# Halving the experts' weights inside the experts' stage of a perceiver layer, without a copy in memory

## The reference

```
logits = router(x @ wqkv.T)                     # N x 8
top_logits, idx = top_k(logits, 2)
scores = softmax(top_logits)
for each row and each of its 2 experts e:
    a, g = split(x_row @ w1[e].T, 2)            # 704 and 704 values
    out_row += score * ((silu(a) * g) @ w2[e].T)
```

## Time and profile before

| | us |
|---|---|
| median of 3 runs | 1886.67 (1884.86 to 1888.04) |
| the profiled execution | 1884.02 |
| its span, first to last instruction | 1882.2 |
| PE busy | 1736.2 (92%) |
| DVE busy | 1387.1 (74%) |
| ACT busy | 1307.0 (69%) |
| POOL busy | 1293.4 (69%) |

### The profile page before, as it was taken

One profiled execution on the slowest core, in us unless ns is written; L12 is line 12 of the kernel. 1 busy time (PEld: TensorE's weight loads), 2 busy tenths in 40 slices (PEclk: granted clock), 3 DMA queues, 4 the chain that ended last, 5 costly groups with the idle time before them and its releaser, 6 DMA issues. The chain is left out here.

```text
span 1882.2 us, 59167 instructions
## 1 busy us (share of the span) xinstructions
PE 1736.2 (92%) x24673; PEld 1146.0 (61%) x24673; DVE 1387.1 (74%) x3579; ACT 1307.0 (69%) x1610; POOL 1293.4 (69%) x669
## 2 busy tenths in 40 slices
PE   6899999999999999999999999999778993699996
PEld 3566666666666666666666666666534672588885
DVE  7788888888888888888888888788766566544443
ACT  5588788888878888878888878888664442233332
POOL 3488888898888888898898888888652100243442
PEclk9999999999999999999999999999898785799998
DMA  8544445444445544445554545554166674688884
GB/s 274 157 119 121 128 113 156 130 127 112 131 117 151 136 129 112 131 117 146 138 132 111 132 117 142 134 138 104 51 215 203 202 236 148 241 248 254 267 245 119
DMA packets 170923, 290.83 MB, mean 155 GB/s; under 512 B 56162, under 2 KB 138466, under 8 KB 170434
## 3 DMA queue, kind: packets, MB, share of 16 engines
q1 hardware_dynamic: 163170, 276.83, 50.6%
q0 software_dynamic: 7488, 10.23, 2.7%
HBM read 169.80 MB, written 33.16 MB: 108 GB/s over the span
## 5 line engine op out<-in xcount | busy, mean ns | idle before, releaser
L420 POOL TENSOR_TENSOR pl<-pT,ph 128x1024 f16<-128x1024 f32 x416 | 881.7, 2132 | 188.4 <-ACT ph L462 188.2
L679 DVE CUSTOM_DVE_ANT_0 junk<-ring,mbias 128x804 bf16<-128x804 f32 x496 | 491.5, 991 | 155.7 <-issue 150.1
L460 ACT ACTIVATE pT<-score,small 128x1024 f32<-128x1024 f32 (+1 forms) x416 | 464.5, 1117 | 68.0 <-PE score L485 34.0
L462 ACT ACTIVATE ph<-score,small 128x1024 f16<-128x1024 f32 (+1 forms) x416 | 464.5, 1117 | 0.0
L883 PE MATMUL ring<-cp,wkp 128*128 128x402 f16 x1536 | 309.0, 338 | 10.2 <-DVE kst L758 3.3
L894 PE MATMUL ring<-wvp,cp 128*128 128x256 f16 (+1 forms) x2496 | 306.3, 274 | 2.9 <-DVE v L664 1.7
L894 PEld LDWEIGHTS ring<-wvp,cp 128*128 128x128 f16 (+1 forms) x2496 | 233.7, 99 | 78.4 <-issue 21.8
L623 POOL TENSOR_TENSOR cp<-cx,cp 128x804 f16<-128x804 f32 x128 | 252.9, 1996 | 21.5 <-ACT cp L792 21.5
L800 ACT ACTIVATE kh<-ring,small 128x402 f16<-128x402 f32 x256 | 155.2, 606 | 154.9 <-PE ring L883 154.9
L908 PE MATMUL ring<-kh,qm 32*128 32x402 f16 x992 | 253.1, 334 | 4.9 <-DVE mx L679 0.3
L507 PE MATMUL o_acc<-v,pl 128*128 128x33 f16 (+1 forms) x3328 | 240.2, 178 | 0.0
(11 more groups left out here) (243 smaller groups left out, 2098.5 us busy)
## 6 DMA issues: line engine op xcount, KB each, us to landing
cx<-in_ctxT SPq DMA_DIRECT2D x32, 1601.0 KB, 6.7
w1p<-wsp SPq DMA_DIRECT2D x24, 1408.0 KB, 8.0
kst<-kh SPq DMA_DIRECT2D x256, 100.5 KB, 2.9
msk<-in_mask SPq DMA_DIRECT2D x64, 400.2 KB, 5.5
kst<-kh SPq DMA_DIRECT2D x256, 99.6 KB, 2.5
wsp<-w_parts SPq DMA_DIRECT2D x24, 704.0 KB, 5.8
w2p<-wsp SPq DMA_DIRECT2D x24, 640.0 KB, 4.3
kst<-kl SPq DMA_DIRECT2D x128, 100.5 KB, 2.7
```

The costliest lines, as they stand in the source:

```text
L420: pool.tensor_tensor(pl[:, u].rearrange("p h q -> p (h q)"), pT[:, u], ph[:, u].rearrange("p h q -> p (h q)"), ALU.subtract).then_inc(pl_r ...
L460: act.activation(pT[0:n, u].rearrange("k (h a q) -> k a h q", a=2, q=S), scored, ACT.Exp, bias=lift[0:n, 0:1], scale=SSCALE)
L462: act.activation(ph[0:n, u].rearrange("k h (a q) -> k a h q", a=2), scored, ACT.Exp, bias=lift[0:n, 0:1], scale=SSCALE).then_inc(exp_done, 1)
L679: dve.tensor_tensor_reduce(junk[:, n % 2], made[:, :, 0:KW], mbias[:, j, 2 * KW * half:2 * KW * half + 2 * KW].rearrange("p (c k) -> p c k ...
```

## The change

The round trip through `wsp` goes. The steps WL, HI, LW and WS leave the five lists of self-attention, with `w_whole` and `w_parts`, and the lists are put into another order throughout. In the experts' stage SP loads whole floats of the tile's expert, 128 x 2 x 1408 and 128 x 6 x 256, into `w1s` and `w2s` (three buffers each), and ACT and DVE halve them there into `w1p` and `w2p`: per tile three pieces of w1 (1024, 1024 and 768 columns) and two of w2 (768 and 768). The pieces of all 24 tiles form one sequence. The first three are done ahead of tile 0, and then the table SPLITS hands out two in each unit of tile 0 and of a paired tile, and one in each unit of a lone tile. `up(i, u)` waits for the low half of its own piece of w1, and `down(i)` for both low halves of w2.

`keep_y` moves from DVE to ACT, at unit 1 of the next tile, and scales with one pointer operand; the constant factor is now multiplied into `wslot` in routing by one more DVE step per block of rows. The memset of `he` moves from DVE to POOL, beside a new one of a part of `w2s`; both wait for the stores of self-attention.

```diff
+STAGES = 3
+W1_PARTS = [slice(4 * P * u, min(4 * P * u + 4 * P, WP)) for u in range(UN)]
+W2_PARTS = [slice(0, UN), slice(UN, FT)]
+PIECES = [("W1", i, n) for i in range(NT) for n in range(UN)]
+for i in range(NT):
+    PIECES[5 * i + 3:5 * i + 3] = [("W2", i, 0), ("W2", i, 1)]
+SPLITS = {}
+for i in range(NT):
+    for u in range(UN):
+        at = UN + sum(len(s) for s in SPLITS.values())
+        SPLITS[i, u] = [q for q in PIECES[at:at + (COUNT[i] if i else 2)] if q[1] < i + WB - (q[0] == "W2" and u < UN - 1)]
...
-SELF_DVE = steps("ZN0 ST0 ST1 ST2 ST3 ST4 N0 ST5 ST6 ST7 ST8 ST9 ST10 ST11 ST12 ST13 ST14 N1 VV0 HS0 VV1 HS1 QL0 QL1 "
...
-                 "LW22 RC12 RC13 RC14 RC15 LW23")
+SELF_DVE = steps("ST0 ST1 ST2 ST3 N0 ZN0 ST4 ST5 ST6 ST7 ST8 ST9 ST10 ST11 N1 VV0 HS0 VV1 ST12 ST13 HS1 ST14 VV2 QL0 "
...
-                        elif kind == "LW":
-                            j = n % 2
-                            dve.wait_ge(w_high, n + 1)
-                            dve.scalar_tensor_tensor(w_parts[:, j, 1], w_whole[:, j], WSCALE, w_parts[:, j, 0], ALU.mult, ALU.subtract).then_inc(w_low, 1)
...
                     def load(i, e):
 
+                        j = i % STAGES
+                        after(sp, w1_low, UN * (i - STAGES + 1))
+                        sp.dma_start(w1s[:, j], a["w1T"][e].rearrange("o (c p) f -> p (o c) f", p=P)).then_inc(w1_in[j], 16)
+                        after(sp, w2_low, 2 * (i - STAGES + 1))
+                        whole = a["w2T"][e].rearrange("o f d -> (o f) d")
+                        sp.dma_start(w2s[:, j, 0:FT - 1], whole[0:(FT - 1) * P].rearrange("(t p) d -> p t d", p=P)).then_inc(w2_in[j], 16)
+                        sp.dma_start(w2s[0:FROWS[-1], j, FT - 1], whole[(FT - 1) * P:F]).then_inc(w2_in[j], 16)
+
+                    sp.wait_ge(w2_clear, 1)
...
+                    def low_w1(i, u):
+
+                        dve.wait_ge(w1_high, UN * i + u + 1)
+                        j, part = i % STAGES, W1_PARTS[u]
+                        dve.scalar_tensor_tensor(w1p[:, i % WB, :, 1, part], w1s[:, j, :, part], WSCALE, w1p[:, i % WB, :, 0, part], ALU.mult, ALU.subtract).then_inc(w1_low, 1)
...
+                    low_w1(0, 0)
                     low_rows(0)
+                    low_w1(0, 1)
+                    low_w1(0, 2)
                     for i in range(NT):
                         gates(i, 0)
                         if i > 0:
                             low_product(i - 1, 2)
+                            low_parts(i - 1, 2)
                         gates(i, 1)
                         low_product(i, 0)
                         if i + 1 < NT:
                             low_rows(i + 1)
-                        if i > 0:
-                            keep_y(i - 1)
+                        low_parts(i, 0)
                         gates(i, 2)
                         low_product(i, 1)
+                        low_parts(i, 1)
...
+                    def high_w1(i, u):
+
+                        j, part = i % STAGES, W1_PARTS[u]
+                        act.wait_ge(w1_in[j], 16 * (i // STAGES) + 16)
+                        after(act, ag_done, UN * (i - WB) + u + 1)
+                        act.activation(w1p[:, i % WB, :, 0, part], w1s[:, j, :, part], ACT.Copy, scale=WSCALE).then_inc(w1_high, 1)
...
+                    def keep_y(i):
+
+                        act.wait_ge(rows_ready, 1 if UPTO[i + 1] <= SOON else 2)
+                        act.wait_ge(y_done, i + 1)
+                        after(act, sc_done, 16 * UPTO[max(i - 1, 0)])
+                        for half in range(COUNT[i]):
+                            h = UPTO[i] + half
+                            act.activation(ys[:, i % 2, half, :], s_ps[:, i % 2, D * half:D * half + D], ACT.Copy,
+                                           scale=wslot[:, h:h + 1]).then_inc(y_kept, 1)
...
+                    high_w1(0, 0)
                     high_rows(0)
+                    high_w1(0, 1)
+                    high_w1(0, 2)
                     for i in range(NT):
                         for u in range(UN):
                             silu(i, u)
                             high_product(i, u)
                             if u == 0 and i + 1 < NT:
                                 high_rows(i + 1)
+                            if u == 1 and i > 0:
+                                keep_y(i - 1)
+                            for kind, q, n in SPLITS.get((i, u), ()):
+                                if kind == "W1":
+                                    high_w1(q, n)
+                                else:
+                                    high_w2(q, n)
+                    keep_y(NT - 1)
```

More of the change, by code:

```diff
@@ L377, in program @@
             first2_in, consts2_in, rows2_in = sem("first2_in"), sem("consts2_in"), sem("rows2_in")
-            w_in, w_out = [sem(f"w_whole_in{j}") for j in range(2)], [sem(f"w_parts_out{j}") for j in range(2)]
-            w_high, w_low = sem("w_high_parts"), sem("w_low_parts")
             stats_made, moments_made = sem("stats_made"), sem("moments_made")
@@ L1242, in _ @@
                             act.activation(xt2[:, n % 2], bank("TU", n)[:, 0:D].rearrange("p (c k) -> p c k", c=DC), ACT.Copy).then_inc(yt_ready, 1)
-                        elif kind == "HI":
-                            e, k, j = n // PIECES, n % PIECES, n % 2
-                            act.wait_ge(w_in[j], 16 * sum(1 if q % PIECES < DC else 2 for q in range(j, n + 1, 2)))
-                            after(act, w_out[j], 16 * (n // 2))
-                            act.activation(w_parts[:, j, 0], w_whole[:, j], ACT.Copy, scale=WSCALE).then_inc(w_high, 1)
                 @block.tensor
@@ L1422, in program @@
             iota_in = sem("iota_in")
-            w1_in, w2_in = ([sem(f"{n}{j}") for j in range(WB)] for n in ("w1_in", "w2_in"))
+            w1_in, w2_in = ([sem(f"{n}{j}") for j in range(STAGES)] for n in ("w1_in", "w2_in"))
+            w1_high, w1_low, w2_high, w2_low, w2_clear = (sem(n) for n in ("w1_high", "w1_low", "w2_high", "w2_low", "w2_clear"))
             he_clear = sem("he_clear")
@@ L1445, in load @@
                     def load(i, e):
-                        j = i % WB
-                        after(sp, ag_done, UN * (i - WB + 1))
-                        sp.dma_start(w1p[:, j].rearrange("p c z f -> p c (z f)"),
-                                     wsp[e, 0:DC].rearrange("o c p z f -> p (o c) (z f)")).then_inc(w1_in[j], 16)
-                        after(sp, y_done, i - WB + 1)
-                        whole = wsp[e, DC].rearrange("o p z f -> (o p) z f")
-                        sp.dma_start(w2p[:, j, :, 0:FT - 1].rearrange("p z t d -> p z (t d)"), whole[:, :, 0:(FT - 1) * D]).then_inc(w2_in[j], 16)
-                        for z in range(2):
-                            sp.dma_start(w2p[0:FROWS[-1], j, z, FT - 1].rearrange("r (h f) -> r h f", h=2),
-                                         whole[:, z, (FT - 1) * D:WP].rearrange("(r h) f -> r h f", h=2)).then_inc(w2_in[j], 16)
-                    for j in range(2):
-                        sp.wait_ge(w_out[j], 16 * (E * PIECES // 2))
+                        j = i % STAGES
[6 more added lines that the diff above has]
+                    sp.wait_ge(w2_clear, 1)
                     sp.wait_ge(te_ready, 1)
@@ L1489, in scatter @@
                                                     ys[:, i % 2, half, :], None, compute_op=ALU.add).then_inc(sc_done, 16)
+                    pool.wait_ge(xn_stored, 16 * NCH)
+                    pool.wait_ge(acc_stored, 16 * NCH + 16)
+                    pool.memset(w2s[:, :, FT - 1], 0.0).then_inc(w2_clear, 1)
+                    pool.memset(he[:], 0.0).then_inc(he_clear, 1)
                     pool.wait_ge(rows_ready, 1)
-                    pool.wait_ge(xn_stored, 16 * NCH)
                     for i in range(2):
                         gather(i)
-                    pool.wait_ge(acc_stored, 16 * NCH + 16)
                     for i in range(NT):
@@ L1504, in _ @@
                 def _(dve):
-                    dve.memset(he[:], 0.0).then_inc(he_clear, 1)
                     count = [0]
@@ L1620, in keep_rows @@
                         step(dve.tensor_copy(wslot[:, lo:hi], high))
-                        dve.tensor_tensor(wslot[:, lo:hi], low, wslot[:, lo:hi], ALU.add).then_inc(rows_ready, 1)
+                        step(dve.tensor_tensor(wslot[:, lo:hi], low, wslot[:, lo:hi], ALU.add))
+                        dve.tensor_scalar(wslot[:, lo:hi], wslot[:, lo:hi], 1.0 / (VSCALE * WSCALE * WSCALE), None, ALU.mult).then_inc(rows_ready, 1)
                     def low_product(i, u):
@@ L1651, in gates @@
                                               ALU.mult).then_inc(he_done, 1)
-                    def keep_y(i):
-                        dve.wait_ge(y_done, i + 1)
-                        after(dve, sc_done, 16 * UPTO[max(i - 1, 0)])
-                        for half in range(COUNT[i]):
```

(18 more changed lines are left out.)

42 lines of the change are left out of this document (15 added, 27 removed), and 40 rows, old and new, of tables (SELF_ACT, SELF_DVE, SELF_PE, SELF_SP).

## The result

The changed kernel takes 1896.41 us (median of 5 runs, 1894.32 to 1898.41) against 1886.67: ratio 1.0052, 95% interval 1.0038 to 1.0067. It is slower, as forecast, by 10 us and not by 18. Its profiled execution took 1897.24 with a span of 1895.4; before it was 1884.0 and 1882.2.

The account below looks back on a forecast made before the run. PE was taken to bound the experts' stage. 1884.0 - 20 (self-attention) + 0.4 (routing) + 38.5 (experts) = 1902.9, plus 2.7 from profiled execution to median: 1905.6, written 1905; 8-in-10 range 1878 to 1924.

Parts of the forecast that it names:

- Self-attention: forecast 20: Self-attention without the halving and in new order: 20 us less, from 5.5 at the tail, 7 in waits, 8 for order.
- the rest of the new order: Self-attention: first normalisation asked for after two exponentials, second products and routing pulled apart; 8 us saved.
- a dependence that stays: End of self-attention: the 6.2 us wait of the last normalisation would remain, keeping the estimate nearer the tail.
- all the idle time: Self-attention: upper bound of the saving, 47 us, all of PE's idle time there.
- Rival A: Faster: self-attention recovers nearly all PE idle time (-38), pieces fall into ACT's idle time (+12); 1861 us, chance 0.17.
- Routing and the start: Routing: one more DVE step per row block, +0.4 us. Experts' start: first pieces delay tiles 0 and 1, +5.
- The period: forecast 34.5: Experts' steady state: three tiles take 34.5 us against 30.9, +3.6, with pieces and `keep_y` in ACT's queue.
- PE reaches its second product before the low half is there in both of the last cases: Experts: for paired after paired and lone after paired tiles, PE waits on DVE's low half and idles a tenth.
- +27 for the stretch: Experts, tile 1's start to tile 22's second product: seven longer periods, one without its second paired tile, add 27 us.
- The late lead: Experts, tiles 16, 19 and 22: first products wait for late low pieces, +2.2 us three times, +6.6.
- Rival C: Slower still: PE's clock in the experts' stage falls with its new gaps, 9.5 us more; 1915 us, chance 0.14.
- Rival B: About the same: lag absorbed, ACT's work alone sets a 31.6 us period, +17 in experts against -20; 1884, chance 0.13.

Follow-up runs that it names:

- the last version: Changed kernel with the low half of unit 2 made earlier on DVE and one extra piece handed out in tiles 4 and 13: 1863.27 us, 0.9874.
- small pieces: Changed kernel halving only 16 columns of each w1 piece and 8 of each w2 row from tile 3 on, loads and waits kept: 1859.94 us, 0.9850.

## Why the prediction was right in its sign, and where it was off

**Self-attention: forecast 20, measured 44.** The removed work was sized about right: 5.5 at the tail and 7 in waits make 12.5, and the kernel without halving gave 13.9. The step that failed is "the rest of the new order ... I put at 8": it is 30.5. It failed twice. Of PE's idle time 29.3 us went (46.9 to 17.6), which the forecast held to be mostly dependences; the 6.2 us wait of the last normalisation, "a dependence that stays", is not among PE's waits of after, the longest of which there is 3.6. And the upper bound, "all the idle time", left out that PE's busy time could shrink: it did by 14.7 us, with the clock from 0.83 to 0.88. This was one of the stated signs of being wrong (35 or more). Rival A's 38 for this stage was nearer to the 44, though by idle time alone it counted 9 too many.

**Routing and the start: forecast +0.4 and +5, measured +7.4 together** (`pr` to the first product of tile 1: 46.3 before, 1588.62 - 1534.93 = 53.7 after). The first product comes 3.4 us later against `pr`, where 2.7 were expected. The other 4 us are tile 1's first product, which waits 5.15 us for its low piece. It did not run "at full clock, 2.6 and not 4.5" in return: it took 4.34.

**The period: forecast 34.5, measured 34.5** where the clock is full, 1679.46 to 1713.95; that is one of three full periods in the first half, and the other two had 36.1. From one first Silu to the next, ACT took 13.1, 9.7 and 11.7 us there (starts 1676.79, 1689.90, 1699.64, 1711.29), where the forecast had 12.7, 10.0 and 11.8. The small terms held: 1.05 and 0.84 for the high pieces (1046 and 830 ns), `keep_y` 0.48 (467 ns). The low pieces were put at about 1.0 and took 1215 and 950 ns. The estimate of 0.47 for `keep_y` agrees as well; it was made from the 0.38 of the earlier trace rows and the 93 ns of the Trainium skill ("ScalarE: Activation LUTs", What ACT_TABLE_LOAD costs). But "PE reaches its second product before the low half is there in both of the last cases" held in one of them only. In tile 8, a paired one behind a paired one, PE came to the second product of tile 7 late by itself, because its first product had waited 1.60 for a low piece of `w1`, a wait that the forecast did not have there. With the low half early the period is 33.6, one more piece ahead makes it 33.0, and only with next to nothing to halve is it 31.1. The forecast's +27 for the stretch is also 1.8 more than its own terms give (7 x 3.6 = 25.2).

**The late lead: forecast +2.2 for tiles 16, 19 and 22.** The wait grew from 1.60 to 4.05, by 2.4, at the place and in the tiles foretold (2.2 in the forecast). What came behind it was not in the sum.

**Rival C, the clock, was no rival but part of the outcome.** It had a chance of 0.14 and a price of 9.5 us; the clock from 1574 to 1870 was 0.92, against the 0.95 below which I said I would be wrong. By the chain, what ran slow after a wait is: twice a second product of 6.00 instead of 4.43, three first products of 5.28 instead of 2.78, second products of 5.47 and 5.24 instead of 4.43, and three smaller first products of 1.94, 2.17 and 2.28 instead of 1.51: 3.1 + 7.5 + 1.9 + 1.9 = 14.4 us. From tile 1's first product to tile 22's second one after has 281.5 us and before 232.5, 48.9 more. The forecast's terms, 25.2 + 6.6 = 31.8, and these 14.4 make 46.2; 2.7 us stay without a name. For a late period (1775.36 to 1816.57) the terms close: 34.5, + 2.4 for the wait, + 2.5 for the first product at 5.28, + 1.0 for the second product and + 0.4 for the smaller first one make 40.8, measured 41.2. The Trainium skill ("TensorE: Matmul & The Clock Gate", HAM oscillation) says that waits between groups of matmuls throw the clock back; the trace agrees in after, where the 24 matmuls behind each wait of 4.05 us took 5.28. It is not so in every run: behind 3.86 us the kernel with `keep_y` on DVE had 5.28, 4.18 and 2.78. The stretch at 1.00 that I set against the rival, PE busy 91%, has no wait of 2 us or more in it.

**The other signs.** PE's largest wait in the stage was to be for `hep`; it is for low pieces of `w1p`, 33.5 us against 9.4, and these waits come 16 times, in the tiles 2, 5, 8, 11 and 14 too. ACT was to be 85 to 90% busy and is 67%. Tile 1's first product was to come 14 us behind the first one and comes 11.6 behind. ACT's wait for the second product, 27.2 us, is there as foretold.

**In sum** the direction followed from PE's stage, as argued, but the 1896 came out as two errors that cancel: 24 us too little given back and 18 too little lost (57.3 against 38.9). That the sum lands so near is luck. Of the 9 us between forecast and median 6 are theirs, the other 3 are how the two profiled executions stand to their medians. Rival B, a period of 31.6 by ACT's work alone, was seen in no kernel that does the whole halving: 33.0 is the shortest.

**What stays open.** Whether the late wait makes the low clock behind it: the three such waits of after all had it, but equal waits in other runs were followed by either level (3.86 us by 5.28 and by 2.78, 2.44 by 4.40 and by 2.78), and no run changes the clock alone. Why the first two periods had 0.95 and the next 1.00 with the same waits of 2.29. How much of the 4 us by which the last version's gain exceeds its period is the second lead piece. And what the new order of self-attention gives with the halving still in it.

## What to carry to other kernels

Work that is moved from a side stage onto engines that feed the bounding one costs its place in their queues, even when they are a third idle: count how far ahead of its use each piece is made, since here one piece made earlier was worth 20 us and a wait moved from one unit or engine to another changed the time by 5 us either way. When a forecast has PE near full clock and adds waits of some microseconds, put slower matmuls behind the waits into the sum, at least in its bounds, rather than into a rival. And removing work from a stage should be tried apart from reordering it: here the order, not the removed work, was most of the gain, and it was there with the old experts' stage too (1841.7, in a kernel without any halving).

## What the runs showed of the hardware

The granted clock was not a function of the waits alone. Second products behind the same wait of 2.29 us took 6.00 at 1619 and 1655 and 4.43 at 1691 and 1725; `keep_y` on DVE, behind 2.23 us, had 5.99 at 1616 and 1722 and 4.42 at 1652 and 1687 between. The same holds for longer waits: behind 3.86 us that kernel had 24 matmuls in 5.28, 4.18 and 2.78, and "small pieces" behind 2.44 had 4.19, 4.40 and 2.78. In the kernels where no late wait of 4 us was left and the low half came early, the clock was 1.00 for 230 us with PE busy 90%.

The start of `pr` varied between profiled runs of nine kernels with the same instructions up to there, from 1530.8 to 1538.8. Half of that is older than self-attention: the same late step of the batch loop on POOL started between 1324.7 and 1328.9 in the same nine. A single profile places the end of such a stage no better than 4 us either way.
